# Turns three steps behind their projections, score rows two steps later, and the next tile normalised ahead of the values' copy

## What is computed

```
x: (4, 1024, 512)      H = 16 heads of 32, E = 16 experts, top 2
mod = silu(c) @ wmod   -> sa, ca, ga, sb, cb, gb per batch
h = layernorm(x) * (1 + ca) + sa
q, k, v = split(h @ W_qkv.T);  q, k = rope(q), rope(k)
p = softmax(causal(q @ k.T / sqrt(32)));  y = p @ v
x = x + ga * (y @ W_o.T)
h = layernorm(x) * (1 + cb) + sb
scores = sigmoid(h @ Wg.T + bias);  top 2, weights divided by their sum
x = x + gb * sum over the chosen experts of w * (silu(h @ W1[e]) @ W2[e])
```

## Time and profile before

| | |
|---|---|
| timed runs, median | 1680.94 us (1679.05 to 1681.72) |
| profiled execution, its own time | 1677.18 us |
| its span, first to last instruction | 1675.4 us |
| busy: PE / PEld / DVE / ACT / POOL | 1424.2 / 1012.4 / 1243.9 / 835.5 / 760.4 us |
| mean granted TensorE clock | 0.943 of full speed |

### The profile page before, as it was taken

How to read it: one execution, slowest core, us unless ns; L and a number is a source line. 1 busy time by engine, 2 the same in 40 slices (tenths; PEclk the granted TensorE clock), 3 DMA queues, 4 the chain that set the end, 5 groups by cost and what they waited for, 6 DMA issues and landing times. The chain is left out here.

```text
span 1675.4 us, 27972 instructions
## 1 busy us (share of the span) xinstructions
PE 1424.2 (85%) x8739; PEld 1012.4 (60%) x8739; DVE 1243.9 (74%) x2932; ACT 835.5 (50%) x1418; POOL 760.4 (45%) x677
## 2 busy tenths in 40 slices
PE   5679998899899889999987998999873999999900
PEld 4556665566566556656655565665341999999800
DVE  3577777687777768777776776778757777777787
ACT  4324646634454763445465434555413666666522
POOL 3245355352434535243453433454525677777500
PEclk9799999999999999999999999999995999999955
DMA  6544444534344453434445342435644454444399
GB/s 211 173 155 151 133 132 102 164 114 158 101 129 126 112 163 114 157 95 133 125 114 164 114 158 90 121 86 164 228 151 167 160 184 157 144 150 141 121 346 382
DMA packets 128529, 255.07 MB, mean 152 GB/s; under 512 B 15632, under 2 KB 67344, under 8 KB 127904
## 3 DMA queue, kind: packets, MB, share of 16 engines
q1 hardware_dynamic: 104192, 184.46, 35.6%
q0 software_dynamic: 13952, 48.25, 8.6%
q10 hardware_dynamic: 10272, 20.97, 3.4%
HBM read 167.60 MB, written 86.02 MB: 151 GB/s over the span
## 5 line engine op out<-in xcount | busy, mean ns | idle before, releaser
L687 ACT ACTIVATE probs<-ring 128x1024 f32<-128x1024 f32 (+3 forms) x384 | 310.1, 811 | 187.7 <-PE ring L541 118.9
L506 PE MATMUL ring<-stack_t 96*128 96x512 f32 (+3 forms) x768 | 297.2, 411 | 24.1 <-DMA stack_t<-stack_dram 15.4
L484 PE MATMUL ring<-w_parts,h_hi 128*128 128x384 f32 x1024 | 275.2, 350 | 9.3 <-DVE neg_max L847 4.0
L1148 POOL TENSOR_TENSOR rope_a<-rope_a,rope_b 128x256 f32<-128x256 f32 x128 | 127.6, 997 | 337.6 <-DVE rope_b L920 337.6
L850 DVE CUSTOM_DVE_ANT_0 ring<-ring,later_b 128x384 f32<-128x384 f32 (+3 forms) x512 | 246.6, 496 | 23.6 <-PE ring L506 22.7
L506 PEld LDWEIGHTS ring<-stack_t 96*128 96x128 f32 x768 | 142.2, 193 | 173.8 <-issue 64.9
L1134 POOL TENSOR_TENSOR prob_sum<-prob_sum,probs 128x1024 f32<-128x1024 f32 (+3 forms) x128 | 229.9, 1796 | 22.8 <-ACT probs L687 21.9
L535 PE MATMUL ring<-stack_t 128*128 128x512 f32 (+3 forms) x768 | 212.6, 359 | 22.7 <-ACT probs L687 12.3
L484 PEld LDWEIGHTS ring<-w_parts,h_hi 128*128 128x128 f32 x1024 | 191.0, 197 | 17.6 <-issue 12.3
L847 DVE TENSOR_REDUCE neg_max<-ring 128x1 f32<-128x512 f32 x256 | 174.6, 682 | 13.5 <-PE ring L506 12.6
L484 PE MATMUL ring<-w_parts,h_lo 128*128 128x384 f32 x512 | 176.4, 345 | 0.0
(11 more groups left out here) (192 smaller groups left out, 2438.5 us busy)
## 6 DMA issues: line engine op xcount, KB each, us to landing
stack_t<-stack_dram SPq DMA_DIRECT2D x384, 128.0 KB, 3.3
stack_dram<-parts SPq DMA_DIRECT2D x64, 512.0 KB, 2.7
w_parts<-w_dram SPq DMA_DIRECT2D x24, 768.0 KB, 7.3
w_sb<-y_dram SPq DMA_DIRECT2D x32, 512.0 KB, 8.6
w_sb<-w SPq DMA_DIRECT2D x22, 512.0 KB, 5.6
x_in<-x SPq DMA_DIRECT2D x32, 256.0 KB, 3.8
x<-x SPq DMA_DIRECT2D x32, 256.0 KB, 3.5
x_dram<-x SPq DMA_DIRECT2D x32, 256.0 KB, 2.6
```

Of the source, the lines that this page charges most:

```text
L484: mm = nc.tensor.matmul(ring[:, BANK[use], 0:384], lhs[:, c, cols], rhs[:, c, :], start=(k == 0), stop=(k == len(products) - 1))
L506: nc.tensor.matmul(ring[:, BANK[use], 0:width], stack_t[0:MROW, i % 2, 0, h, qt * P:qt * P + P], stack_t[0:MROW, i % 2, 1, h, kc * 512:kc ...
L687: nc.scalar.activation(probs[:, step % PROBS, :, q0:QC], ring[:, bank:bank + 2, q0:QC], ACT.Exp)\
L1148: nc.gpsimd.tensor_tensor(rope_a[:, t % 2, :], rope_a[:, t % 2, :], rope_b[:, :], ALU.add)\
```

## The change

Four tables and the place of one question in ACT's loop are changed. No instruction is added or removed.

```diff
-TURN = {step + 2: it for step, it in PROJECT.items()}
+TURN = {step + 3: it for step, it in PROJECT.items()}
 NORM_A = {norm_step(b, t): (b, t) for b in range(B) for t in range(NT)}
-NORM_B = {step + (1 if bt[0] else 2): bt for step, bt in NORM_A.items()}
-NORM_C = {step + 1: bt for step, bt in NORM_B.items()}
-MAX_FROM = {i: STEPS * (i - 1) + 1 for i in range(GROUPS)}
+NORM_B = {step + 1: bt for step, bt in NORM_A.items()}
+NORM_C = {step + (1 if bt[0] else 2): bt for step, bt in NORM_B.items()}
+MAX_FROM = {i: STEPS * (i - 1) + 3 for i in range(GROUPS)}
@@ ACT's walk along the timeline
                         if 0 <= step < STEPS * GROUPS:
                             exponentials(step)
-                        if step in NORM_B:
-                            normalise(*NORM_B[step])
...
                         if step in NORM_C:
                             first_norm(*NORM_C[step])
+                        if step in NORM_B:
+                            normalise(*NORM_B[step])
                         if step in TURN:
                             high_parts(*TURN[step])
```

## The result

Four timed runs of the changed kernel gave 1699.02 to 1701.57 us, median 1699.61; the kernel before, in runs beside them, had 1681.33. The ratio is 1.0115 with a 95% interval of 1.0094 to 1.0136. The forecast was 1667, with 1650 to 1682 as its range. The profiled execution took 1701.57 us (span 1699.8, mean clock 0.926 of full speed; before 1677.18, 1675.4 and 0.943).

A forecast was written before the change was run, and what follows sets the result against it. It took PE to bound the middle (976.7 of 1055.2 us busy) and a chain of waits the lead-in; -8.2 and -6 us gave -14.2 from 1677.2, 1663 profiled, so 1667 for the median, range 1650 to 1682.

The forecast's parts named there:

- Turns in the middle: Middle: 47 PE waits for POOL's rotary sum vanish at 0.48 us each, saving 22.6 us (16.5 to 38).
- The rival that gave the middle nothing: Middle: PE, early by 0.5 us, meets exponentials, maxima and banks; only the lead-in's gain stays, 1675 us; chance 0.20.
- The maxima's waits in step 10: Middle, step 10: half of PE's waits for `max_tok` and behind `h_lo` go, -3.6 us (-7.3 to 0).
- The new wait for `max_tok`: Middle, combining in step 3: PE newly waits 0.4 us in each of 15 groups, +6 us (0 to +21).
- The spread: Middle, steps 4 and 12: ACT's spread of maxima makes columns wait in 15 groups, +5 us (0 to +10).
- Banks: Middle, projection steps using six banks: one more projection wait for maxima of about 0.5 us per group, +7 us (0 to +19).
- Lead-in: Before the first score columns: fewer waits for `x_hat`, parts and turns, -6 us all told (-13 to -2).
- the 3.9 us of waits for `x_hat`: Lead-in: PE transposes' waits for normalisation behind the values' copy on ACT; 3.9 of 8.3 us were to go.
- The trip through DRAM: Lead-in: from turn to needing rows 12.4 us; an earlier ACT copy takes some 1.8 us off second and third rounds.
- Clock: Lead-in: 7 us more at half speed costs 3.5 us, inside the bounds; the skill's rule would leave 2 to 3 gained.
- The slower rival: Middle: 30 spreads of maxima in short steps; at 0.9 us of PE waiting each, +8 us, 1689 us; chance 0.10.
- the signs by which the prediction would have called itself wrong: Middle: waits for `rope_a` return as waits for `probs`, or L535 waits for the spread over 0.6 us in each group.

The follow-up runs named there:

- y_start: Changed kernel with DVE's combining of maxima at the end of the step before and group 0's turns two steps behind their projections; 1678.34 us, ratio 0.9995.
- y_max_comb: Kernel before with score rows two steps later and maxima combined at the end of the step before, turns and normalisation as before; 1680.57 us, ratio 1.0014.
- e_turn: Kernel before with only the turns moved, to three steps behind their projections; 1705.78 us, ratio 1.0170.
- x_comb: Changed kernel with DVE's combining of maxima moved to the end of the step before; 1683.74 us, ratio 1.0029.
- e_max: Kernel before with only score rows, combining and turn of maxima moved two steps later; 1695.80 us, ratio 1.0104.
- x_pool: Changed kernel with POOL's sum of probabilities at n = 4 cut to the last 8 columns, leaving out part of the denominators; 1690.21 us, ratio 1.0069.
- x_best: Changed kernel, combining at the end of the step before, maxima's turn and spread in steps 11 and 5, group 0's turns two steps behind; 1701.21 us, ratio 1.0155.
- x_comb_far: Changed kernel with combining at the end of the step before and PE's turn of maxima with ACT's spread in steps 11 and 5; 1712.97 us, ratio 1.0189.

## Why the prediction was wrong

It forecast -14.2 us in the profile and +24.4 came. By its own steps:

- **Turns in the middle, -22.6.** This is the term that failed by most. The waits went as foreseen (none in the middle), and their worth failed: alone the late turns cost 19.6 us of middle, and with late rows and early combining they are worth nothing that could be measured (y_start against y_max_comb, 1678.34 and 1680.57). A wait of 0.3 us on PE is not work. What PE met in its place in e_turn were banks held by maxima (18.5 us, 2.7 before), parts (10.6, 2.4 before) and the low part of a tile (9.3). The rival that gave the middle nothing came nearest, at 0.20; it too forecast a faster kernel.
- **The maxima's waits in step 10, -3.6.** Those for `max_tok` are gone. But they were the sign of the very standstill, in the kernel before, that the change then made general. Those behind `h_lo` only moved, to columns: 6.0 us in 6, where rows and turns of maxima had 4.3.
- **The new wait for `max_tok`, +6.** This is the second step that failed, and without it the kernel is 0.3% slower and not 1.2 (x_comb). It sized the combining by its rows in step 1, 0.6 us for three instructions with POOL idle, and moved it to step 3, where POOL's rotary sum starts 0.04 us before. The place was right (16.0 us in 15, all in step 4), the total was not. Ten of the waits are 0.28 to 0.46 us, the forecast's 0.4, but by luck: they are no longer than what POOL's rotary sum adds to L861, 0.54. The rest are 1.98 us four times, where the sum of probabilities holds the cast too, and group 0's 4.57. Moved away, the combining gave back 17.5 us of middle. The bound of 21 held that.
- **The spread, +5.** 9.7 us in 7, near the upper bound of 10. Three of them are 2.8 us, and not because steps are short: on ACT the spread stands behind the scalings of a tile in step 12 of the groups that normalise.
- **Banks, +7.** Projections wait less for maxima (3.0 us against 7.7), but score rows wait for them 11.2 us in 6 and columns 6.2 in 12 (before 1.0 and 2.7). The three kinds together are 20.4 us and were 11.4: 9 more, the size about right, the place wrong.
- **The wait for `h`** had no term. A step of DVE between two that moved met POOL too: 12.2 us in 3.
- **Lead-in, -6.** -2.6. (Its own terms, -6.3 and -2 with the 1.8 us of work put off given back, add up to -6.5.) Of the 3.9 us of waits for `x_hat` 0.9 went. The first and third landings came at 49.5 and 77.4, where the prediction took about 48.7 and 72.2; the waits are 4.6, 4.5 and 6.6 us, not 4, 1 and 6. The trip through DRAM was to get 1.8 us shorter and got 1.6 longer. The late turns were counted as a gain of time; y_start, with group 0's turns back at two steps, has its first columns 6.8 us earlier than x_comb. All of the lead-in's gain is the score rows put off (e_max, -8.2).
- **Clock.** Its bound was for the lead-in alone. There the time at 1.2 GHz rose from 20.5 to 34.1 us, and the 2.6 us gained are the 2 to 3 that the sentence on the Trainium skill's rule (TensorE: Matmul & The Clock Gate, "HAM oscillation") gave. The direction agrees in the parts too: e_turn's lead-in waits 25.0 us for the DMA and stands 41.0 at that level, e_max's 2.6 and 13.7. But the number may be luck, for the late read-back alone took 3.2 us more than before. x_pool walks the changed kernel's lead-in with 20.5 us at that level; its third landing was 1.5 us later and its first columns 0.6 earlier. By that the 13.6 us more cost the lead-in 0.6 to 2.1 us, an estimate from one execution each. How the missing 3.4 us divide stays open.

The middle's time at 1.2 GHz rose from 31 to 75 us. What that costs can only be estimated, from pairs of single executions: x_best against x_comb_far, same idle time, 34.2 us less at the lower level, 13.8 us faster, 0.40 us for each; y_max_comb against y_start, 20.5 us less and 1.0 less idle, 4.8 faster, 0.19 for each. By that 44 us would be 8 to 18 of the 26, and PE's idle time grew by 16.5. In group 6 it reads so, in a stretch behind the wait of 1.98 us (us, then each engine's busy us, the clock third from the end):

```profile
550.80:554.20 3.40, 3.40 (x15) 3.33 (x15) 1.63 (x7) 1.64 (x3) 0.00 (x0) 0.50 0.13 54
```

The slower rival, the spread in short steps, had the right sign and the wrong mechanism. Of the signs by which the prediction would have called itself wrong, neither came: PE waits less for `probs` than before (10.7 us against 12.3), and for the spread in seven places only. It named no sign for a combining that takes longer at its new place.

## What to carry to other kernels

Before small VectorE instructions on SBUF are moved, look at what GpSimd runs at their new place: their price is then the rest of GpSimd's instruction, and not their own length alone. A row that shows a duration at one place bounds it there only; the long exceptions of the same line (L869's 2.28 us here) tell what else can happen. And a short wait on the busiest engine is often slack that others live on: what it is worth is measured by removing it, never by adding up its idle time.

## What the runs showed of the hardware that was not expected

- A 128x16 cast of 0.18 us took 1.23 beside a GpSimd addition of 1.26, and 0.18 beside one of 0.22 (the changed kernel and x_pool). The standstill has the length of what is left of the other's instruction, whatever the size of one's own: the `tensor_tensor` of 0.17 us took 0.71 beside an addition of 0.72 us, and the L976 of 0.75 us, begun 0.43 us into a sum of 2.52, took 2.64.
- A short standstill can cost more than its length. x_pool took 4.3 us from L861 and L866 in the middle (26.6 to 22.3) and 6.6 from DVE's busy time, and the median fell by 9.4. Moving the combining (x_comb) took 6.4 us from the two (26.6 to 20.2) and 17.5 from the middle, with 16.0 of PE's waiting for `max_tok`, of which 3.7 had another cause.
- Two executions in which PE idled 106.9 us in the middle took 1097.7 and 1083.9 us for it, with 92 and 58 us at the lower clock level (x_comb_far and x_best, which differ in group 0's turns alone).
- A read-back of six pieces took 7.1 to 8.9 us to land whole in the four traces in which two loads of 1 MB were issued from another queue before its last piece, and 3.5 to 4.5 in the other twelve.
